# Channel stage of a fused conv block: the first product with token rows, and the row norm that follows it

## What is computed

```
t = _gn(x).reshape(B, H*W, 48)            # the flat NCHW memory, cut into rows of 48
t = gelu(gelu(t @ W1 + b1))               # W1: 48 x 16
x1, x2 = t[..., :8], t[..., 8:]
n = layernorm(x2) * gamma + beta          # over 8 values
sp = depthwise 3x3 conv(n) + dw_b         # n seen as (8, 128, 128)
ch = 1x1 conv(n) + pw_b
out = (x1 * (sp * ch)) @ W2 + b2          # 8 x 48
x = x + out
```

## Time and profile before

| | us |
|---|---|
| three runs | 2916.2, 2926.2, 2931.5 (median 2926.2) |
| the profiled execution | 2921.2 |
| its span, first to last instruction | 2919.4 |
| DVE busy | 1618.7 (55%) |
| ACT busy | 1085.7 (37%) |
| GpSimd busy | 249.8 (9%) |
| channel stage, from the first affine (2639.2) to the end | about 280 |
| mean granted TensorE clock, of full speed | 0.935 |

### The profile page before, as it was taken

How to read it: one execution, slowest core, us unless ns; L and a number is a source line. 1 busy time by engine, 2 the same in 40 slices (tenths; PEclk the granted TensorE clock), 3 DMA queues, 4 the chain that set the end, 5 groups by cost and what they waited for, 6 DMA issues and landing times.

```text
span 2919.4 us, 47382 instructions
## 1 busy us (share of the span) xinstructions
PE 2489.0 (85%) x18076; PEld 2176.8 (75%) x18076; DVE 1618.7 (55%) x3797; ACT 1085.7 (37%) x2617; POOL 249.8 (9%) x244
## 2 busy tenths in 40 slices
PE   2989999999999899999999806999999998006886
PEld 2989949949943699999999806999999997002443
DVE  3323233233232555885578874568855788686565
ACT  3433253253257344444444423444344443002221
POOL 1000000000000540000000140000000000354110
PEclk9999999999999999999999957999999999557898
DMA  8830000003002300000000093000000000673223
GB/s 153 148 66 1 1 1 1 1 0 87 1 0 53 78 1 1 2 2 1 1 1 2 12 255 80 1 1 1 2 1 1 1 2 6 193 277 87 86 86 87
DMA packets 51672, 130.17 MB, mean 45 GB/s; under 512 B 9120, under 2 KB 34048, under 8 KB 44896
## 3 DMA queue, kind: packets, MB, share of 16 engines
q1 hardware_dynamic: 48352, 113.92, 16.2%
q10 hardware_dynamic: 2976, 13.34, 1.6%
q0 software_dynamic: 128, 0.01, 0.0%
HBM read 76.91 MB, written 50.33 MB: 44 GB/s over the span
## 4 chain that ended last, share of the span: by engine, by line
PE 83%; DMA 7%; DVE 6%; issue 2%; ACT 1%; POOL 1%; SPq 0%; DVEq 0%; ACTq 0%; POOLq 0%
PE bank L923 17%; PE bank L924 15%; PE bank L926 15%; PE bank L830 13%; PE bank L884 11%; PE bank L845 3%; PE bank L835 3%; DMA flat_rows<-work 2%; DMA work<-saved 2%; PE bank L968 2%; DVE work L322 2%; PE bank L1026 1%; DMA work<-in_x 1%; DMA saved<-image 1%; PE bank L959 1%
## 5 line engine op out<-in xcount | busy, mean ns | idle before, releaser
L1209 DVE TENSOR_SCALAR bank<-image,scan_bias 112x128 f32<-112x128 f32 x2032 | 712.1, 361 | 354.4 <-ACT image L714 332.7
L714 ACT COPY image<-bank 112x128 f32<-112x128 f32 x2032 | 586.7, 289 | 796.7 <-PE bank L926 765.5
L923 PE MATMUL bank<-image,scan_wt 112*112 112x128 f32 x4064 | 816.5, 282 | 32.3 <-ACT image L695 17.4
L924 PE MATMUL bank<-image,scan_wt 112*112 112x126 f32 x4064 | 770.9, 271 | 0.0
L926 PE MATMUL bank<-image,scan_wt 112*112 112x126 f32 x4064 | 770.0, 270 | 0.0
L923 PEld LDWEIGHTS bank<-image,scan_wt 112*112 112x112 f32 x4064 | 557.2, 175 | 42.9 <-ACT image L695 27.9
L924 PEld LDWEIGHTS bank<-image,scan_wt 112*112 112x112 f32 x4064 | 581.7, 176 | 0.0
L926 PEld LDWEIGHTS bank<-image,scan_wt 112*112 112x112 f32 x4064 | 578.5, 176 | 0.0
L621 ACT ACTIVATE work<-image,gn_shift,gn_scale 48x567 f32<-48x567 f32 (+5 forms) x384 | 332.5, 898 | 346.0 <-PE bank L835 219.4
L830 PE MATMUL bank<-work 112*128 112x192 f32 x2304 | 424.0, 332 | 10.0 <-issue 10.0
L830 PEld LDWEIGHTS bank<-work 112*128 112x128 f32 x2304 | 375.3, 193 | 11.7 <-issue 11.2
(11 more groups left out here) (137 smaller groups left out, 1636.6 us busy)
## 6 DMA issues: line engine op xcount, KB each, us to landing
work<-saved SPq DMA_DIRECT2D x64, 384.0 KB, 8.5
saved<-image SPq DMA_DIRECT2D x10, 1536.0 KB, 21.7
flat_rows<-work ACTq DMA_DIRECT2D x32, 384.0 KB, 7.5
image<-flat_rows SPq DMA_DIRECT2D x4, 3072.0 KB, 14.7
out<-image SPq DMA_DIRECT2D x8, 1536.0 KB, 8.0
saved<-image SPq DMA_DIRECT2D x12, 768.0 KB, 10.1
band<-in_x SPq DMA_DIRECT2D x16, 384.0 KB, 5.5
work<-in_x SPq DMA_DIRECT2D x16, 384.0 KB, 5.5
```

What stands on the lines that cost most here:

```text
L714: nc.scalar.copy(line(g, along_w, at), state_bank(g, done)).then_inc(s_state[g], 1)
L923: mm(dst, wt[:, 1], src, start=False, stop=False, skip_group_check=True)
L924: mm(dst[:, 1:J2, :], wt[:, 0], src[:, 0:J2 - 1, :], start=False, stop=False, skip_group_check=True)
L1209: v.tensor_scalar(state_bank(g, done), line(g, along_w, src), scan_bias[:, 3 * layer + kind:3 * layer + kind + 1], None, ALU.add).then_inc ...
```

## The change

`hidden` now takes four products a group. Each has 128 turned tokens of `x_t` (97 rows, 128 columns) as its stationary operand and moves W1 (97 by 32), so the result has token rows and 32 hidden columns, and lands side by side in `bank[2 + g // 4]`. The turning back, its copies, its semaphores and `after` are gone. The second gelu writes from `hid_t` straight to `hid`. TensorE waits for the four first gelus before it fills the banks anew. Row norm waits for the second gelu; its deviation becomes a tensor_scalar of the 128 sums and a tensor_tensor over 1024 values (one more link); its last addition reads with a stride and writes in order. GpSimd builds its small weight tables with `band_tmp[0]` as scratch in place of `s1`.

```diff
--- before.py
+++ after.py
@@ -70,7 +70,7 @@
 N_GATE = 6 + 2 * G
 N_SCAN_DMA = 2 + 6 * 10
 N_BAND = G * 3 * 5
-MLP_LINKS = 10
+MLP_LINKS = 11
 EARLY = 10
 
 
@@ -265,9 +265,6 @@
         s_xt_v = sem("s_xt_v")
         s_hid = sem("s_hid")
         s_gelu = sem("s_gelu")
-        s_hid_t = sem("s_hid_t")
-        s_hid_a = sem("s_hid_a")
-        s_hid_v = sem("s_hid_v")
         s_ln = sem("s_ln")
         s_ln_a = sem("s_ln_a")
         s_gt_p = sem("s_gt_p")
@@ -320,12 +317,6 @@
             i0 = image6[src, ds(bp, 1), :, ds(q * PER * BLK + m * BLK, BLK), :, a]
             i1 = back[m][src, :].rearrange("p (s k j q) -> p s k j q", s=2, k=BLK, q=2)[:, :, :, :, a]
             return eng.tensor_tensor(o[:, :, :, :, half], i0.rearrange("p g s k j -> p (g s) k j"), i1, ALU.add)
-
-        def hidden_views(i):
-
-            return (hid[:, i * 512:(i + 1) * 512].rearrange("p (g t c) -> p t g c", g=4, t=4),
-                    bank[2 + i][:, :].rearrange("p (t g c) -> p t g c", t=4, g=4))
-
 
         TAPS = [(LO, 0, 0, 1), (LO, 1, 0, 0), (HI, 0, 0, 2), (HI, 1, 0, 1), (LO, 1, 1, 2), (HI, 0, 1, 0)]
 
@@ -551,18 +542,18 @@
             pool.dma_start(w1_sb[96:97, HID:2 * HID], b1).then_inc(s_gate_const, 16)
 
             pool.wait_ge(s_band, N_BAND)
-            nc.gpsimd.tensor_copy(s1[:, 0:WQ], ident[:, 0:WQ]).then_inc(s_band, 1)
+            nc.gpsimd.tensor_copy(band_tmp[0][:, 0:WQ], ident[:, 0:WQ]).then_inc(s_band, 1)
             n = N_BAND + 1
             for c in range(1, G):
                 pool.wait_ge(s_band, n)
-                nc.gpsimd.tensor_tensor(s1[:, 0:WQ], s1[:, 0:WQ], ident[:, c * WQ:(c + 1) * WQ],
+                nc.gpsimd.tensor_tensor(band_tmp[0][:, 0:WQ], band_tmp[0][:, 0:WQ], ident[:, c * WQ:(c + 1) * WQ],
                                         ALU.add).then_inc(s_band, 1)
                 n += 1
             pool.wait_ge(s_band, n)
             for o in range(G):
-                nc.gpsimd.tensor_scalar(pw_k[:, o, :], s1[:, 0:WQ], pwr_sb[:, o:o + 1], None, ALU.mult)
+                nc.gpsimd.tensor_scalar(pw_k[:, o, :], band_tmp[0][:, 0:WQ], pwr_sb[:, o:o + 1], None, ALU.mult)
             for e in range(TOK):
-                last = nc.gpsimd.tensor_scalar(w2_k[:, e, :], s1[:, 0:WQ], w2r_sb[:, e:e + 1], None, ALU.mult)
+                last = nc.gpsimd.tensor_scalar(w2_k[:, e, :], band_tmp[0][:, 0:WQ], w2r_sb[:, e:e + 1], None, ALU.mult)
             last.then_inc(s_band, 1)
 
             with pool.Fori(0, NB // 2) as t:
@@ -756,7 +747,7 @@
                     act.wait_ge(s_hid, b * GROUPS + 4 * (i + 1))
                     nc.scalar.activation(hid_t[:, i * 512:(i + 1) * 512], bank[2 + i][:, :], ACT.Gelu).then_inc(s_gelu, 1)
                 act.wait_ge(s_gelu, b * 5 + 4)
-                nc.scalar.activation(hid_t, hid_t, ACT.Gelu).then_inc(s_gelu, 1)
+                nc.scalar.activation(hid, hid_t, ACT.Gelu).then_inc(s_gelu, 1)
 
             def take_turned(b, first, dst):
                 for i in range(2):
@@ -765,9 +756,6 @@
 
             def mlp(b, more):
 
-                for i in range(2):
-                    act.wait_ge(s_hid_t, b * 4 + (i + 1))
-                    nc.scalar.copy(*hidden_views(i)).then_inc(s_hid_a, 1)
                 for g in range(0, 4 if more else 0, 2):
                     take_tokens(b + 1, g)
                 act.wait_ge(s_ln, b * 2 + 1)
@@ -949,7 +937,7 @@
 
             pe.wait_ge(s_gate_const, 16 * 4)
 
-            def tokens(b, g0, g1, after=True):
+            def tokens(b, g0, g1):
 
                 def turn_tokens(g):
                     if g >= 2:
@@ -962,10 +950,10 @@
 
                 def hidden(g):
                     pe.wait_ge((s_xt_a, s_xt_v)[g % 2], b * (GROUPS // 2) + (g // 2 + 1))
-                    if after and g % 8 == 0:
-                        pe.wait_ge((s_hid_a, s_hid_v)[g // 8], b * 2)
-                    lanes = slice(g % 4 * 2 * HID, (g % 4 + 1) * 2 * HID)
-                    last = mm(bank[2 + g // 4][lanes, :], w1_sb, x_t[g % 2][0:97, :], start=True, stop=True)
+                    for t in range(4):
+                        o = (g % 4 * 4 + t) * 2 * HID
+                        last = mm(bank[2 + g // 4][:, o:o + 2 * HID], x_t[g % 2][0:97, t * 128:(t + 1) * 128],
+                                  w1_sb, start=True, stop=True)
                     last.then_inc(s_hid, 1)
 
                 turn_tokens(g0)
@@ -977,13 +965,8 @@
             def mlp(b, more):
 
 
-                pe.wait_ge(s_gelu, b * 5 + 5)
-                for i in range(4):
-                    for t in range(4):
-                        o = i * 512 + t * 128
-                        last = nc.tensor.transpose(bank[2 + i][:, t * 128:(t + 1) * 128], hid_t[:, o:o + 128], ident)
-                    last.then_inc(s_hid_t, 1)
                 if more:
+                    pe.wait_ge(s_gelu, b * 5 + 4)
                     pe.wait_ge(s_xn, b + 2)
                     tokens(b + 1, 0, EARLY)
 
@@ -1028,7 +1011,7 @@
                            start=True, stop=True).then_inc(s_proj, 1)
 
             pe.wait_ge(s_xn, 1)
-            tokens(0, 0, GROUPS, False)
+            tokens(0, 0, GROUPS)
             pe.wait_ge(s_band, N_BAND + G + 1)
             with pe.Fori(0, NB - 1) as b:
                 mlp(b, True)
@@ -1329,14 +1312,10 @@
             def row_norm(b, i):
 
                 if i == 0:
-                    for k in range(2, 4):
-                        dve.wait_ge(s_hid_t, b * 4 + (k + 1))
-                        v.tensor_copy(*hidden_views(k)).then_inc(s_hid_v, 1)
-                    dve.wait_ge(s_hid_a, 2 * b + 2)
-                    dve.wait_ge(s_hid_v, 2 * b + 2)
+                    dve.wait_ge(s_gelu, b * 5 + 5)
                     link(v.tensor_reduce(s1, x2, AX, ALU.add))
-                    link(v.scalar_tensor_tensor(out=dev_v, in0=s1.unsqueeze(2).to_broadcast(per_w), scalar=-1.0 / G,
-                                                in1=x2, op0=ALU.mult, op1=ALU.add))
+                    link(v.tensor_scalar(s1, s1, -1.0 / G, None, ALU.mult))
+                    link(v.tensor_tensor(dev_v, x2, s1.unsqueeze(2).to_broadcast(per_w), ALU.add))
                 elif i == 1:
                     link(v.tensor_tensor(dev2, dev, dev, ALU.mult))
                     link(v.tensor_reduce(s2, dev2_v, AX, ALU.add))
@@ -1347,9 +1326,8 @@
                     link(v.tensor_tensor(dev2_v, dev_v, s5.unsqueeze(2).to_broadcast(per_w), ALU.mult))
                 elif i == 3:
                     link(v.tensor_tensor(dev2_v, dev2_v, gam_sb.unsqueeze(1).to_broadcast(per_w), ALU.mult))
-                    v.tensor_tensor(spm_v.rearrange("p q c w -> p q w c"),
-                                    dev2.rearrange("p (q w f) -> p q w f", q=NQ, f=G),
-                                    bet_sb.unsqueeze(1).unsqueeze(1).to_broadcast([128, NQ, WQ, G]),
+                    v.tensor_tensor(spm_v, dev2.rearrange("p (q w f) -> p q f w", q=NQ, f=G),
+                                    bet_sb.unsqueeze(1).unsqueeze(3).to_broadcast([128, NQ, G, WQ]),
                                     ALU.add).then_inc(s_ln, 1)
 
             def mlp(b, more, even_more):
```

## The result

The changed kernel is slower: median 2946.63 us of 6 runs (2943.63 to 2956.17) against 2924.05 us of 6 runs of the kernel before beside it, ratio 1.0101 with the 95% interval 1.0084 to 1.0118. (The ratio on record is not the quotient of the two medians, which is 1.0077; either says slower.) The forecast was 2907, the range 2890 to 2928: wrong in sign, and outside the range. The main mechanism is that of the rival *The clock falls, slower*, whose size was given as 2967; image 0 also went as in the rival *The collision stays*.

What follows compares the result with a forecast made beforehand. It took the channel stage's chain of waits as the bound, with GpSimd's add holding DVE's row norm. Terms -16.5 + 0.5 - 1.4 - 1.9 = -19.3 us gave 2901.9 for the profiled execution, 2907 for the median; range 2890 to 2928.

Steps and rivals of the forecast that it cites:

- The clock falls, slower: Rival, token loops: 32-column products leave the clock at 0.50, 44 periods 1.4 us longer, +60 us, 2967; chance 0.10.
- The collision stays: Rival, image 0: the last row norm addition comes late and GpSimd's add still holds it; -2.8 us, 2923; chance 0.17.
- The first product, turned: Token loops: eight passes at 0.105 us, 0.93 against 0.98 us a group; -1.4 us over 36 periods (bounds +2 and -22).
- Image 0, -16.5 us: Image 0's row norm: its last addition starts 2.4 us ahead of GpSimd's add, so it is not held; -16.5 us.
- The delay from affine to add: Channel stage: GpSimd's add is tied to the affine's end, 13.66 us later for image 0 and 13.71 for image 1.
- Images 1 and 2, +0.5 us: Row norm of images 1 and 2: still held by GpSimd's add; 0 to +0.35 us each, +0.5 taken for both.
- the upper end of that term: Images 1 and 2: the small scale is held and the tensor_tensor follows it; up to +0.35 us each.
- The last image, -1.9 us: Last image, no add: the row norm reduction starts 2.1 us earlier and row norm pays 0.25 us; -1.9 us.
- the bounds with up to 0.6: The 16 periods of the start: they shift affine and add alike, worth up to 0.6 us, not in the sum.

Runs made afterwards that it cites:

- wide128: The changed kernel with W1 padded with zeros so each turned product moves 128 columns instead of 32: 2899.68 us, ratio 0.9938 to the kernel before.
- after: The changed kernel itself, measured beside the kernel before: 2946.63 us against 2924.05, ratio 1.0101.
- wide64: The changed kernel with W1 padded with zeros so each turned product moves 64 columns instead of 32: 2949.10 us, ratio 1.0108 to the kernel before.
- wide96: The changed kernel with W1 padded with zeros so each turned product moves 96 columns instead of 32: 2917.66 us in one run (kernel before 2926.81).
- wide128_hold: The changed kernel with 128 moved columns and GpSimd's add of b2 waiting for the previous image's row norm: 2876.88 us, ratio 0.9854 to the kernel before.
- wide128_hold_oldnorm: The changed kernel with 128 moved columns, GpSimd's add waiting for the previous image's row norm, and the old row norm: 2876.18 us, ratio 0.9855.
- one_product: The changed kernel issuing only the last of each group's four products, with 128 columns (three quarters of tokens not computed): 2897.48 us in one run.

## Why the prediction was wrong, point by point

**The step that failed** is "The first product, turned": 8 passes at 0.105 us each, -1.4 us over 36 periods. The price of a pass was read where the clock was 1.00, and was nearly right there: 0.81 us for eight in the chain, 0.10 each. (The whole period was forecast at 1.51 and is 1.27 at 1.00: the transposes take 0.45 and not 0.57, and the product 0.81 and not 0.93, with its 0.1 for hand-overs.) That the loop would hold this clock was taken from two short stretches, 1.8 us of L871 and the rise under L984. Neither is a loop of transposes and 32-column products that goes on for 30 us, and in that loop the clock was 0.50 throughout, so a pass took 0.19 us and a period 2.43, 0.88 more than before where 0.04 less was forecast. wide128 shows it: with the same passes and loads and the clock at 1.00 in image 0's tokens it is 47 us faster.

In the Trainium skill, "TensorE: Matmul & The Clock Gate", Part 4, the full clock does not engage for transposes, which do not count as busy in the same way. The loop of the change, where a third of the period is transposes (0.88 of 2.43) and the rest 32-column products, stayed low, which is in line with it. It is no proof, since the loop before had as large a share of transposes (0.57 of 1.55) and ran at 1.00. The rise under L984's 16 transposes does not fit the rule taken as absolute, and I let that one row overrule it. Both should have stood as evidence of the same weight, which is a chance far over 0.10.

**Image 0, -16.5 us.** The working was sound and its premise fell with the clock. L1329 started 1.3 us behind the add, not 2.4 us ahead, and was held for 12.05 us. Of these 3.7 us, 1.4 are the second gelu, which ended 1.7 us after the affine and not 0.3, since the last tokens of image 0 came late. The other 2.3 are DVE's waits for the transposes of image 1's groups 3 and 5 (0.24 and 2.05 us). This is what *The collision stays* had described; it had named the late transposes and the low clock at their start, but not the gelu. The stretch is 36.95 us in both kernels, as the add ends it either way. In wide128 the clock is high, L1330 starts 2.2 us ahead of the add, and the stretch is 22.84 us, -14.1.

**The delay from affine to add** held: 13.66 and 13.71 us before, 2693.91 - 2680.34 = 13.57 and 2753.43 - 2739.90 = 13.53 after.

**Images 1 and 2, +0.5 us.** The hold fell on the operation that the upper end of that term names, the small scale, but was 6.75 us long and not 9 to 10. The 16 output additions ended 16.1 us after the affine (2755.99), not 13.0, so row norm came later into the same add; the granted clock was 0.54 from 2740 to 2744, under their first products. The Trainium skill, "SBUF — State Buffer", section "Who interferes with whom", has a tensor_scalar contend in a two-port mode and a reduction never, and the trace agrees: 6.75 us for an operation of 0.23, while L1316 just ahead of it took its usual 1.22 under the same add (from 2753.43). Which port mode the scale ran in, no trace here shows. Image 1's L1318 ended 2765.22 - 2739.90 = 25.3 us after the affine, as L1338 did before. From there to L975 it was 21.3 us instead of 15.2: that is the clock again, and all of the +6.1 of that row.

**The last image, -1.9 us.** The term held, though no row of the table shows it alone. The gap between the last output addition and the reduction was 2.2 us (2865.83 to 2867.99) and is gone; from the reduction to L992 / L975 it is 11.43 us instead of 11.06. That makes -1.9. It lies in the row of +0.1, where the stretch up to that addition took 2.0 us more. The -1.5 of the last row is something else: the 48 banded products behind L975 took 6.04 us there against 7.12, the same instructions with a clock that rose sooner. The addition that reads with a stride takes 1.99 us and not 1.89.

**The price of the low clock.** The rival had 2.9 us a period, from L984's 0.22 us a pass; it was 2.43, with 1.55 / 8 = 0.19 a pass. At 0.88 us more a period its 44 periods make 39 us, not 60. The 12 ahead of image 0 were all paid: +10.7 in the first row. The 6 in image 0 were hidden, since GpSimd's add ends that stretch either way. For the 26 of images 1 and 2 the five rows behind that stretch add up to +17.7 us instead of 23; a few of these loops ran at 1.00 (2803.06 above). So +26.9 in the stage, and +22.6 in the medians.

**The sum without the clock.** wide128 came out 20.3 us under the kernel before, the forecast's sum was -19.3. That they agree so well is in part luck. The freed row norm of image 0 gave 14.1 us and not 16.5, with 1.8 us of a held affine in it. The periods were 0.29 us shorter and not 0.04, and the stretch from the first affine to the second, which the sum left in the bounds with up to 0.6, gave 3.2 us (26.50 against 29.67).

## What to carry over

A cheaper form of a product is priced together with the clock that it will run at, and that is read only from rows of the same mix over the same length; where it ran long enough only in another mix, the low clock belongs in the range. A loop in which TensorE is never idle can stand at half clock (32.00 of 32.00 us busy at 0.50), and moving more columns with the same loads can then be faster than moving fewer (2899.68 with 128, 2946.63 with 32). An operation of GpSimd that holds DVE's two-input work can be moved by one more wait to where DVE doesn't need it: that gave the kernel before 30 us, while a faster TensorE freed image 0's addition and brought a hold of the affine instead.

## What the runs showed that was not expected

- Granted clock 0.50 with TensorE busy 32.00 of 32.00 us, in after and wide64; 1.00 with 19.00 of 19.00, in the kernel before. Being busy throughout went with either level.
- The same mix at 1.00 for 16 us and at 0.50 for 24 us in wide96. What raises or keeps the clock is not settled by these runs.
- A scale of 128 elements, 0.23 us, held for 6.75 to 10.40 us. Its size is no protection.
- A scale of 6144 elements is held too: the affine takes 3.47 us when free, 5.28 in wide128, 4.83 in wide128_hold, 6.05 in wide128_hold_oldnorm, and 12.23 in one_product, where it started 1.4 us behind the add.
